# Moving the key weights' product with a bias ahead of the last row of matrix products at the end of setup

## What the reference computes

```python
Q = jnp.einsum('btx,dx->btd', text, Wq) + bq
K = jnp.einsum('bpx,dx->bpd', features, Wk) + bk
scores = jnp.einsum('btd,bpd->btp', Q, K) * scale
attn = jax.nn.softmax(scores, axis=-1)
attended = jnp.einsum('btp,bpd->btd', attn, features)
```

## Time and profile before

| what | value |
|---|---|
| median of 3 runs | 1991.98 us (1991.7, 1991.98, 1994.03) |
| the profiled execution | 1995.47 us |
| its span in the trace | 1993.7 us |
| mean granted TensorE clock over the span | 0.996 |
| PE busy | 98% of the span |
| DVE, ACT, POOL busy | 52%, 37%, 36% of the span |
| first instruction of PE in stage A | 105.69 us |

### The profile page before, as it was taken

How to read it: one execution, slowest core, us unless ns; L and a number is a source line. 1 busy time by engine, 2 the same in 40 slices (tenths; PEclk the granted TensorE clock), 3 DMA queues, 4 the chain that set the end, 5 groups by cost and what they waited for, 6 DMA issues and landing times.

```text
span 1993.7 us, 37551 instructions
## 1 busy us (share of the span) xinstructions
PE 1957.0 (98%) x14030; PEld 1295.8 (65%) x14030; DVE 1037.5 (52%) x2012; ACT 742.6 (37%) x1560; POOL 724.9 (36%) x719
## 2 busy tenths in 40 slices
PE   8999999999999999999999989999999999999998
PEld 3488888885666666666666645666576676666665
DVE  5655545534555555555555663434444355656554
ACT  5421111222555555555555661111111134444441
POOL 0000000111565566565556550101101236666662
PEclk9999999999999999999999999999999999999999
DMA  7433333333222222223322454334333495665661
GB/s 235 145 90 119 96 109 99 123 97 81 66 68 68 66 69 65 65 69 85 97 70 66 101 134 136 112 99 116 103 113 111 135 285 175 204 213 185 209 206 61
DMA packets 317583, 236.43 MB, mean 119 GB/s; under 512 B 248270, under 2 KB 285134, under 8 KB 313004
## 3 DMA queue, kind: packets, MB, share of 16 engines
q1 hardware_dynamic: 290364, 222.47, 38.5%
q10 hardware_dynamic: 27120, 12.60, 2.4%
HBM read 177.01 MB, written 57.94 MB: 118 GB/s over the span
## 4 chain that ended last, share of the span: by engine, by line
PE 87%; DVE 2%; DMA 2%; ACT 2%; issue 1%; SPq 1%; POOL 0%; DVEq 0%; ACTq 0%
PE a_pr L723 14%; PE c_x_ps L1592 10%; PE b_kv_ps L1122 9%; PE b_kv_ps L1126 9%; PE d_f_ps L2030 8%; PE b_s_ps L1163 7%; PE b_o_ps L1178 7%; PE c_t_ps L1613 7%; PE d_a_ps L1815 3%; PE a_pr L719 3%; PE b_mx_ps L1138 3%; PE c_f_ps L1642 2%; PE d_s_ps L1783 2%; DMA t_scratch<-c_tT 1%; DVE c_y2T L1553 1%
## 5 line engine op out<-in xcount | busy, mean ns | idle before, releaser
L925 POOL TENSOR_TENSOR b_probT<-b_exp,b_probT 128x448 f16<-128x448 f32 (+2 forms) x256 | 265.5, 1039 | 296.4 <-ACT b_probT L989 296.3
L503 POOL TENSOR_TENSOR cT<-ctx_raw,cT 128x375 f16<-128x375 f32 x256 | 222.4, 889 | 133.6 <-ACT cT L498 132.6
L723 PE MATMUL a_pr<-a_yT,proj_q_p 128*128 128x256 f16 x2016 | 223.2, 273 | 0.0
L723 PEld LDWEIGHTS a_pr<-a_yT,proj_q_p 128*128 128x128 f16 x2016 | 197.3, 98 | 23.4
L1126 PE MATMUL b_kv_ps<-wkv_p,cT 128*128 128x384 f16 (+1 forms) x1152 | 210.6, 325 | 0.0
L1059 DVE TENSOR_REDUCE b_nmax<-b_mx_ps 112x2 f16<-112x974 f32 x128 | 149.6, 1169 | 109.5 <-PE b_mx_ps L1138 109.4
L1122 PE MATMUL b_kv_ps<-cT,wkv_p 128*128 128x375 f16 x1152 | 199.0, 323 | 0.0
L1163 PE MATMUL b_s_ps<-b_qT,b_kT 96*128 96x448 f16 (+5 forms) x768 | 190.6, 356 | 3.2 <-DMA b_qT<-b_nrow 2.2
L1178 PE MATMUL b_o_ps<-b_probT,b_v 128*128 128x448 f16 (+5 forms) x768 | 187.3, 351 | 4.5 <-POOL b_probT L925 4.5
L987 ACT ACTIVATE b_exp<-b_s_ps 128x448 f32<-128x448 f32 (+2 forms) x256 | 137.9, 539 | 128.5 <-PE b_s_ps L1163 121.9
L2030 PE MATMUL d_f_ps<-wo_early,d_y3T 128*112 128x512 f16 x768 | 174.9, 381 | 0.0
(11 more groups left out here) (209 smaller groups left out, 2796.8 us busy)
## 6 DMA issues: line engine op xcount, KB each, us to landing
ctx_raw<-in_ctx_t SPq DMA_DIRECT2D x32, 1500.0 KB, 7.2
d_cn_raw<-in_ctx_nat SPq DMA_DIRECT2D x32, 512.0 KB
b_qT<-qk_scratch SPq DMA_DIRECT2D x32, 336.0 KB, 4.5
o_scratch<-b_o SPq DMA_DIRECT2D x128, 84.0 KB, 2.0
qk_scratch<-a_heads SPq DMA_DIRECT2D x70, 144.0 KB, 2.1
d_cn_raw<-in_ctx_nat SPq DMA_DIRECT2D x16, 476.0 KB
x_scratch<-c_x SPq DMA_DIRECT2D x14, 512.5 KB, 3.5
tiles_in<-in_x SPq DMA_DIRECT2D x14, 512.0 KB, 4.3
```

Source lines behind the costliest of these rows:

```text
L503: pool.tensor_tensor(cT[:, p, 1, k, 0:S], ctx_raw[:, k, :], cT[:, p, 0, k, 0:S], ALU.subtract).then_inc(split_lo, 1)
L723: last = mm(pr[:, n % PR, 0:GT * P], w[:, b, k, at * P:(at + 1) * P], yT[:, g % 2, a, k, :], start=(x == 0 and k == 0), stop=(x == 2 and k ...
L925: pool.tensor_tensor(pT[0:m, c, 1, :], ex[0:m, i % 2, :], pT[0:m, c, 0, :], ALU.subtract).then_inc(p_lo, 1)
```

## The change

On PE the product of `wk_p` with its bias is made in front of row 15 of the products, where the constant `C_AT` = 15 puts it, and not behind that row. It keeps its wait (`m_lo` of at least 10), its bank and its semaphore. On ACT the copy to `c_parts` moves with it: it now stands in front of the copy of row 15 to `Mt`, not behind that row's pieces. DVE's program is unchanged; its addition into `c_col` still stands at its end.

```diff
-                    U_AT, TILES_AT = 14, (10, 12)
+                    U_AT, C_AT, TILES_AT = 14, 15, (10, 12)
...
+                            if i == C_AT:
+                                act.wait_ge(b_done, 1)
+                                act.activation(c_parts.rearrange("p k l -> p (k l)"), m_ps[:, 1, 0:2 * KD], ACT.Copy,
+                                               scale=1.0 / WS).then_inc(b_read, 1)
                             act.wait_ge(m_done, i + 1)
...
-                        act.wait_ge(b_done, 1)
-                        act.activation(c_parts.rearrange("p k l -> p (k l)"), m_ps[:, 1, 0:2 * KD], ACT.Copy,
-                                       scale=1.0 / WS).then_inc(b_read, 1)
...
+                            if i == C_AT:
+
+                                pe.wait_ge(m_lo, BANKS + 2)
+                                columns_of(wk_p, 0, 1, b_done)
                             pe.wait_ge(m_lo, i - BANKS + 1)
...
-                        pe.wait_ge(m_lo, BANKS + 2)
-                        columns_of(wk_p, 0, 1, b_done)
```

## The result

The changed kernel took 1996.07 us in the median of 20 runs (1993.58 to 1999.12), the kernel before 1993.03 us in 20 runs of the same comparison (1990.2 to 1997.43). The ratio is 1.0014, with a 95% interval of 1.0009 to 1.0020: 1.8 to 4.0 us slower, inside the 0.2% that I had called the limit of what can be told, though with this many runs it can be told. The forecast was +1.9 us and 1993.9 us, in a range up to 1996.8. Of the 2.2 us between 1993.9 and 1996.07, 1.05 us is the base: the forecast started from a median of three runs, 1991.98 us, and the kernel before came to 1993.03 in 20.

A forecast was written before the change was run, and what follows sets the result against it. TensorE, busy 98% of the span, was taken to bound the kernel. Setup's end +2.3 us and stage A -0.4 us sum to +1.9 us on a median of 1991.98 us: 1993.9 us, range 1990.8 to 1996.8 us.

The forecast's parts named there:

- The small matmuls and ACT's copy move at no cost: End of setup: PE's moved wait is long met, and ACT's 0.18 us copy for c lies in its idle time.
- A fall costs row 15 1.68 us: Row 15, now behind the small matmuls, meets a clock fall to 0.50, priced as in row 14: 1.68 us.
- The first rival: The clock doesn't fall under row 15; setup ends 0.63 us later, time 1991.7 to 1992.6 us; chance 0.22.
- The tail lost its cover, 0.63 us: Row 15's copy, pieces, u_bc copies and s0, before hidden under the product with wk_p, now are not: 0.63 us.
- Setup's end, +2.3 us: End of ACT's part goes from 105.39 to 107.69: 1.68 us from the clock, 0.63 us from lost cover.
- Stage A, -0.4 us: Stage A's start: faster transposes against a fall behind PE's longer idle stretch, bounds -0.9 and +0.8 us, taken as -0.4 us.
- The sum, +1.9 us: Whole kernel: setup's end +2.3 us and stage A -0.4 us give +1.9 us.
- From one trace to a median: The profiled execution was 3.5 us above the median; the +1.9 us was added to the median, 1991.98 us.
- The bounds of the forecast's case: Part or all of a fall under row 15: +1.0 to +3.5 us, 1993.0 to 1995.5 us, chance 0.68.
- The rival that the clock stays down: All of row 15 runs at half clock, costing 5.18 us more: +5.8 us, 1997.8 us; chance 0.05.

The follow-up runs named there:

- the pieces first: Changed kernel, but ACT and DVE make row 15's five pieces of stage A's weights before waiting for row 15; ratios to the kernel before 0.9995 and 1.0000.
- the twelve: Twelve matmuls added in PE's wait near 481 us: kernel before 0.9993, changed 1.0011, changed with the pieces first 0.9999, both products spread with the pieces first 1.0000.
- the block of 256: Changed kernel, but both products with a bias stand in front of row 14, 256 small matmuls in one block; ratio to the kernel before 1.0011.

## Why the prediction was right

- **The small matmuls and ACT's copy move at no cost.** Right: c's copy ends at 97.56 in ACT's idle time, and neither PE nor ACT waits for anything new.
- **A fall costs row 15 1.68 us.** Right: 10.17 us between the two copies is 5.18 + 3.31 for the block + 1.68. That the block brings it is shown: none of the seven products that were spread (c alone, and both in three traces) has a fall behind it, while with c as a block in front of row 15 five of six traces have one. The first rival, which spared row 15, is real too: the sixth, the second with the pieces first, has none. All three traces of the changed kernel had it, that with the twelve at a cost of 1.5 us.
- **The tail lost its cover, 0.63 us.** Right, and shown by the pieces first: 2.96 us against a predicted 2.98, and 1.64 with them out of the way. But 0.63 is small only because the old tail had itself paid for a fall, with 0.85 us under the `diag` matmuls; without that fall the same sum gives 1.5 us.
- **Setup's end, +2.3 us.** The way to stage A grew by 2.27 us.
- **Stage A, -0.4 us.** From its start to its first L723, now L726, it took 117.82 - 105.69 = 12.13 us before and 119.20 - 107.53 = 11.67 us after: -0.46 us. The transposes, the first of them at full clock, won 0.8 us up to the first product (4.32 to 3.50 us), and the fall behind the idle stretch took 0.4 back under the 48 products behind them (7.97 to 8.34 us).
- **The sum, +1.9 us**, was small against +2.8 us, at the interval's lower edge. In the traces compared it is +1.8 us, from row 13's copy to the first L723 (L726). So the terms fit the traces, and what fell short is the step from one trace to a median.
- **From one trace to a median.** The traced execution of before had both falls, and its own 1995.47 us lay above 16 of the 20; the fastest of the 20 took 1990.2 us, and the changed kernel's fastest 1993.58. From row 13's copy to the first L723 the traces of before and after have the same clock's loss, 5.1 us. But over the whole kernel the runs beside each other have more in the changed one: 11.5 against 8.6 us (mean clocks 0.9943 in 8 runs and 0.9957 in 32), and with the twelve in both 9.5 against 8.6 us (0.9953 and 0.9957, in 12 runs each). Those 2.9 and 0.9 us are not in the traces' setups. Executions of before that miss a fall which those of the changed kernel meet would explain it, and where such a one misses the fall at the end of setup, the tail costs 1.5 us, not 0.63. It stays argued: a mean clock tells no place, the second difference is hardly more than these means scatter, and both traces with the old order, before and before with the twelve, had both falls (21.34 and 21.37 us).
- **The bounds of the forecast's case**, +1.0 to +3.5 us, do not follow from the terms: 2.3 - 0.9 and 2.3 + 0.8 are +1.4 and +3.1 us. The range was wide enough for the median to lie in it, at 0.7 us from its upper end, so the range's hold owes something to luck.
- **The rival that the clock stays down**, 1997.8 us, was not what decided: row 15's fall held 3.2 us or a little more in both traces (98.20 to 101.50, 97.80 to 101.00). Two of the 20 runs were as long as 1999 us, from causes not seen.

## What to carry to other kernels

Before moving a block of small matmuls on TensorE, look at what runs behind it: the price of the clock's fall is paid by the work that the fall meets. Here row 15, dense work, paid 1.68 us, while the small matmuls and idle time paid nothing. And ask what the moved block used to cover: the last row's drain on the other engines was free only while PE had something behind that row. Small matmuls could be spread between big ones at no cost here, but whether that or any change of 0.1% helps has to be read from many runs, since where a fall comes differs from one to the next. The mean clock of each run is on record beside its time, and tells what a single trace can't: how much half clock a kernel meets on average.

## What the runs showed of the hardware

- Matmuls of one or two columns are as fast at half clock. 128 of them take 3.3 us at 1.00, 26 ns each, and the last 48 of the block of 256, at 0.50, take 1.28 us (90.27 to 91.55), 27 ns each. 128 of them between 24 of 512 columns add just their own time: 8.48 against 5.18 us.
- A block of 128 small matmuls brings a fall behind it, with PE busy throughout, but not always: behind the u block (both products in front of row 14 left aside) it came in seven of ten traces. It was missing in the first with the pieces first, in that with the pieces first and the twelve, and in that with c left out.
- The place moves between executions: the fall began 88.7 - 87.5 = 1.2 us behind the end of the u block before, and 0.9 and 0.7 us behind it in the changed kernel's two traces. The Trainium skill ("TensorE: Matmul & The Clock Gate", Part 1) says that the monitor runs free of the kernel, so the place is run-variable. These places agree with it. It may not be chance alone, though: the three traces with the pieces first and u as a block each miss exactly one of the two falls, not the same one in each, with a way to stage A of 20.60 us every time, and none of the changed kernel's three misses one.
- A fall also came behind a short idle stretch of PE, in some executions: at stage A's start in four of the nine traces with 2.3 to 2.4 us of idle PE before it (not in that with c spread), in none of the three with 1.09 us; and behind the 2.21 us near 481 us in six of ten, in none of the four in which the wait was filled.
